# First tiles begun behind the first chunk's shift, the second chunk's maxima moved into them

## The chip, the cores and the metric

The kernel runs on one core of one Trainium2 chip. The metric is the device time of one execution in microseconds (us). Engines are named as in the profile: PE is TensorE, DVE VectorE, ACT ScalarE, POOL GpSimd, SP SyncE (which here only issues DMAs).

## The reference

A block of a transformer over T = 4096 rows of D = 256, with 16 heads of 16:

```
x = x + attn(layernorm(x));  x = x + ffn_fp8(layernorm(x))
attn:  q, k, v = split(x @ Wqkv + b)
       soft = softmax(q k^T * scale + causal mask) v                (per head, 4096 x 4096)
       state_t = retention * state_{t-1} + Gamma * (v_t k_t^T) * scale ;  stp_t = (W_static + state_t) q_t
       alpha = sigmoid(gelu(x @ w1 + b1) @ w2 + b2)
       y = alpha * soft + (1 - alpha) * stp ;  return y @ out_w + out_b
```

Softmax with its maxima and the recurrence over 4096 steps are what the change touches.

## The kernel before

The program has three blocks: a prologue (layernorm, projections, the first maxima), the attention block, and a last block (merge, output projection, FFN). The change is in the attention block.

**Groups, chunks, tiles.** The 16 heads are four groups of four. The 4096 queries are eight chunks of 512 (`CH`), taken in the order `ORDER = (3, 4, 5, 6, 7, 2, 1, 0)`; `s` is the place in that order. Chunk c attends to key tiles of 128 keys, 4(c + 1) of them, so a group has 144 tiles (`TILES`): 16 for chunk 3, 20 for chunk 4, and so on. A tile computes four heads' scores on PE (step `scores`, L1349), their exponentials on ACT (L1465, 128x512 each), and two tiles later the product with the values on PE (`values`, L1376), into one PSUM bank for the chunk.

**Maxima and the shift.** The softmax subtracts a maximum per query before the exponential. It is found ahead: step `max` has PE form scores the other way round (L1311), and DVE reduces two banks at a time (L1512). One such reduction is a *pair*: two `max` steps, one for each half of the partitions. Chunk c has 16(c + 1) `max` steps, so 32 pairs for chunk 3 and 40 for chunk 4. Four PSUM banks hold two pairs. When a chunk's last pair is in, DVE folds them (`fold`, L1517), PE turns the result (`shift_turn`, L1434), DVE splits it in two f16 rows (`shift_split`, L1524 and L1527), and SP copies these into `Q_st` with four DMAs of 2 KB, eight rows each (L1159). The first `scores` of the chunk wait for those DMAs (`shift_loaded`).

**The recurrence.** 64 units for a group, in 16 batches of four. SP loads each unit's value rows, broadcast to all partitions (`v_exp`, 256 KB, L1125); POOL multiplies by k (L1219); ACT scales (`scale`, L1474); POOL adds, DVE scans a batch (`scan`, L1547), POOL weighs with q, and every second batch PE has a `burst` of 40 matmuls into one bank. A `lag` (L1385, L1481, L1209) is a small product for every fourth batch.

**The order.** Every engine walks the same list of steps and does its own part of each. `first_steps()` makes the list of the entrance, `group_steps()` that of a group, tile by tile, from a string of letters: S a score, M a `max` step, v and w the halves of the values, V both, R the recurrence's steps, U small moves:

```python
PLAIN_TILE = "USSMMvSSMMw"
BURST_TILE = "USSMMRMMSSMMV"
SCAN_TILE = "USSRvSSMMw"
LAG_TILE = "USSMMVSSMMR"
```

`recurrence_steps()` says at which tile each scan, burst, scale and v load stands. The `max` steps run `AHEAD` = 144 steps (two chunks, 3 and 4) ahead of the tiles: a group's tiles reduce the chunks from the third on and then the next group's first two. Only for group 0 the entrance must do chunks 3 and 4. Chunk 3's maxima are formed in the prologue; chunk 4's 40 pairs are in `first_steps()`, before tile 0 of group 0. SP's part of the entrance is, in this order: the k, q and v rows of the first batch and eight `v_exp`, `V_first` (values of the first five chunks, 680 KB), the queries of chunks 5 and 6, `K_st` and `V_g` for the long chunks, the queries of chunk 7, and then the first chunk's shift rows. All of these go through one queue (`q1`).

Keys lie in `K_first` (first five chunks) and `K_st`, whose rows between the data must hold the constant `SHIFT_UNIT`: POOL fills all of `K_st` at the block's start (L1283) before its first product, and DVE clears the output bank (L1554).

Of the kernel before, what the change touches and what calls it, by code (L numbers as in the profile page):

```python
# [52 lines left out]
ORDER = (3, 4, 5, 6, 7, 2, 1, 0)  # L53
# [5 lines left out]
TILES = sum(KEY_TILES)  # L59
# [69 lines left out]
def transfers(name):  # L129
    return 1 if name[0] == "v" else STACK_LOADS  # L130
# [14 lines left out]

def recurrence_steps(last):

    period = LAST_PERIOD if last else PERIOD
    moves, slots = {}, {}

    def add(at, t, *step):
        at.setdefault(max(t, 0), []).append(step)

    for B in range(N_BATCHES):
        t = period * B + SLOT_AT
        if B % 2 == 1:
            add(slots, t, "burst", 0, B // 2)
        for k in range(BATCH):
            if not (last and B + 2 >= N_BATCHES):
                at, when = (slots, t) if B % 2 == 1 else (moves, t + 1 + k)  # L160
                add(at, when, "scale", 0, BATCH * (B + 2) + k)
            if not (last and B + 3 >= N_BATCHES):
                add(moves, t + V_AFTER + k, "v_load", 0, BATCH * (B + 3) + k)
        if not (last and B + 1 >= N_BATCHES):
            add(slots, t, "scan", 0, B + 1)
    for b in range(1, N_SWEEPS + (0 if last else 1)):
        add(moves, period * (SWEEP_BATCHES * b - 5) + SLOT_AT + KQ_AFTER, "kq_load", 0, b)
        add(slots, period * (SWEEP_BATCHES * b - 3) + SLOT_AT + LAG_AFTER, "lag", 0, b)
    return moves, slots


def first_steps():

    loads = [("load", 0, name, n) for name in EARLY for n in range(transfers(name))]

    steps = [("load_units", 0, 0)] + [x for x in loads if x[2] not in (f"q{ORDER[0]}", f"q{ORDER[1]}", "k_first")]
    release = None
    for s, n in ITEMS[:AHEAD]:
        if s > 0:
            steps.append(("max", 0, s, n))  # L180
        if release and n == 8:
            steps.append(release)
        if s > 0 and n == MAXES[s] // 4:
            steps += [("lag", 0, 0, 2), ("lag_evac", 0, 0, 2)]
        if n == MAXES[s] - 1:
            steps += [("fold", 0, s), ("shift_turn", 0, s, s)]
            release = ("shift_split", 0, s, s)
    if release not in steps:
        steps.append(release)
    steps += [("scale", 0, n) for n in range(BATCH)] + [("scan", 0, 0)]  # L190
    steps += [("scale", 0, BATCH + n) for n in range(BATCH)]
    steps += [("v_load", 0, 2 * BATCH + n) for n in range(BATCH)]
    return steps


def group_steps(last, pending, turns, used):

    steps = []
    todo = [(0,) + x for x in ITEMS[AHEAD:]] + ([] if last else [(1,) + x for x in ITEMS[:AHEAD]])
    rotation = list(range(S_BANKS))  # L200
    moves, slots = recurrence_steps(last)

# [49 lines left out]
    for s in range(NCH):  # L252
        for kt in range(KEY_TILES[s]):
# [87 lines left out]
def preln_attention_ffn_kernel(nc, x, wqkv, bqkv, out_w, out_b, w_static, lam, gamma, gate_w1,  # L341
                               gate_b1, gate_w2, gate_b2, ffn_wt, ffn_b, out):
    ctx = ExitStack()
    with ctx:
# [711 lines left out]
        with att:  # L1056
# [20 lines left out]
            with nc.Block() as block:  # L1077
# [115 lines left out]
                def _(pool):  # L1193
# [100 lines left out]
                def _(pe):  # L1294
# [160 lines left out]
                def _(act):  # L1455
# [44 lines left out]
                def _(dve):  # L1500
# [460 lines left out]
```

## Time and profile before

| | before |
|---|---|
| median of 3 runs | 1769.96 us (1768.66 to 1770.38) |
| the profiled execution | 1767.19 us |
| its span in the trace | 1765.5 us |
| attention block's first instructions | about 162.5 us |
| first exponential (tile 0 of group 0) | 211.44 us |
| busy in the span | PE 1625.4 (92%), DVE 1534.4 (87%), ACT 1394.8 (79%), POOL 1219.2 (69%) us |
| granted TensorE clock, mean | 0.955 |

The span is what the trace shows from the first to the last instruction; the execution's own time is 1.7 us longer. Busy shares are means over the program: the stretches below tell what holds the work in each. In a row of the timeline the number in brackets is the engine's idle time before it, and what ended it. A clock of 0.50 is 1.2 GHz, 1.00 is 2.4 GHz.

### The profile page before, as it was taken

How to read it: one execution, taken by the hardware profiler on the slowest of the kernel's cores; microseconds unless marked ns; L12 is line 12 of the kernel's file. 1: busy time of each engine (PE TensorE's matmuls, PEld its weight loads, DVE VectorE, ACT ScalarE, POOL GpSimd, SP SyncE). 2: the span in 40 equal slices, each digit the busy share in tenths (PEclk: the TensorE clock that was granted, in tenths of full speed). 3: DMA queues.
4: the chain of work that ended last, by engine and by line, in shares of the span. 5: the costliest groups of instructions: out<-in, count | busy, mean ns of one | idle time of the engine just before them, and what ended most of it. 6: DMA issues, size and time to landing. Idle time of an engine off the chain costs nothing. (4 is left out here: it accounts for less than half of the span.)

```text
span 1765.5 us, 44702 instructions
## 1 busy us (share of the span) xinstructions
PE 1625.4 (92%) x17582; PEld 583.6 (33%) x17582; DVE 1534.4 (87%) x1744; ACT 1394.8 (79%) x2839; POOL 1219.2 (69%) x1151
## 2 busy tenths in 40 slices
PE   5995699999999999999999999999999999999655
PEld 3541123233333332333333233233333332333532
DVE  6668989999899999998999999988999999940688
ACT  3651288998987899989888989998888889899234
POOL 3102497778777777787777777877778888880555
PEclk9995599999999999999999999999999999999886
DMA  5784343142212422232124222322242321200712
GB/s 162 252 254 144 77 108 87 58 99 75 74 60 82 112 70 76 73 81 77 63 79 111 65 84 70 98 60 71 85 115 64 97 73 60 69 16 11 244 48 95
DMA packets 115347, 163.22 MB, mean 92 GB/s; under 512 B 30081, under 2 KB 57793, under 8 KB 115137
## 3 DMA queue, kind: packets, MB, share of 16 engines
q1 hardware_dynamic: 112608, 158.74, 30.7%
q8 instruction: 137, 2.24, 0.6%
q10 hardware_dynamic: 2528, 1.64, 0.3%
q14 instruction: 74, 0.60, 0.1%
HBM read 121.87 MB, written 38.01 MB: 91 GB/s over the span
## 5 line engine op out<-in xcount | busy, mean ns | idle before, releaser
L1512 DVE TENSOR_REDUCE pmax<-PS 128x2 f32<-128x1024 f32 (+2 forms) x1120 | 1204.3, 1130 | 84.5 <-PE PS L1311 66.8
L1465 ACT ACTIVATE probs<-PS 128x512 f32<-128x512 f32 (+3 forms) x2304 | 1149.8, 575 | 155.5 <-PE PS L1349 76.5
L1376 PE MATMUL PS<-probs,V_g 128*17 128x256 f32 (+3 forms) x5064 | 395.8, 385 | 4.1 <-ACT o_t L1486 3.7
L1219 POOL TENSOR_TENSOR v_exp<-v_exp,k_rows 128x512 f32<-128x512 f32 x256 | 322.5, 1289 | 26.5 <-DMA v_exp<-qkv_t 26.2
L1349 PE MATMUL PS<-Q_st,K_st 50*128 50x512 f16 (+3 forms) x1408 | 288.8, 364 | 8.0 <-ACT probs L1465 6.6
L1261 POOL TENSOR_TENSOR state<-odd,q_rows 128x514 f32<-128x514 f32 x256 | 282.0, 1134 | 6.1
L1311 PE MATMUL PS<-K_st,Q_st 48*128 48x512 f16 (+3 forms) x1408 | 272.6, 357 | 0.3
L1376 PE MATMUL PS<-probs,V_first 128*17 128x256 f32 (+2 forms) x3296 | 264.9, 393 | 2.2 <-ACT o_t L1486 2.2
L1349 PE MATMUL PS<-Q_st,K_first 50*128 50x512 f16 (+3 forms) x896 | 194.1, 379 | 11.9 <-ACT probs L1465 6.0
L1311 PE MATMUL PS<-K_first,Q_st 48*128 48x512 f16 (+1 forms) x832 | 178.8, 391 | 19.6 <-DVE pmax L1512 19.4
L1250 POOL COPY carry<-odd 128x4 f32<-128x4 f32 x64 | 12.1, 188 | 252.7 <-DVE odd L1547 252.7
L1349 PEld LDWEIGHTS PS<-Q_st,K_st 50*128 50x128 f16 x1408 | 80.3, 93 | 295.4 <-ACT probs L1465 240.8
L1229 POOL TENSOR_TENSOR pairs<-pairs,v_exp 128x512 f32<-128x512 f32 x128 | 162.8, 1294 | 0.0
L1376 PEld LDWEIGHTS PS<-probs,V_g 128*17 128x17 f32 x5064 | 84.0, 95 | 185.6 <-issue 110.7
L1474 ACT ACTIVATE pairs<-v_exp,decay 128x256 f32<-128x256 f32 x256 | 128.6, 543 | 9.7 <-POOL v_exp L1219 9.7
L1349 PEld LDWEIGHTS PS<-Q_st,K_first 50*128 50x128 f16 x896 | 51.8, 93 | 208.9 <-ACT probs L1465 158.2
L1376 PEld LDWEIGHTS PS<-probs,V_first 128*17 128x17 f32 x3296 | 54.7, 95 | 144.2 <-issue 89.8
L1255 POOL TENSOR_TENSOR odd<-odd,pairs 128x512 f32<-128x512 f32 x64 | 96.7, 1510 | 5.0
L714 PE MATMUL PS<-xn_t,w_parts 128*128 128x512 f16 x336 | 84.0, 409 | 9.2 <-DVE xn_t L896 9.1
L1547 DVE TENSOR_TENSOR_SCAN odd<-decay_x,sums 128x516 f32<-128x516 f32 x64 | 82.2, 1285 | 10.9 <-POOL sums L1240 10.9
L1240 POOL TENSOR_TENSOR sums<-sums,pairs 128x512 f32<-128x512 f32 x64 | 82.9, 1296 | 5.0
L1409 PE MATMUL PS<-state,sum_e 128*32 128x256 f32 x1024 | 77.5, 394 | 0.0
(194 smaller groups left out, 1488.5 us busy)
## 6 DMA issues: line engine op xcount, KB each, us to landing
v_exp<-qkv_t SPq DMA_DIRECT2D x256, 256.0 KB
qkv_t<-proj SPq DMA_DIRECT2D x24, 512.0 KB, 4.7
qk_parts<-parts SPq DMA_DIRECT2D x16, 512.0 KB, 5.5
Q_st<-qk_parts SPq DMA_DIRECT2D x192, 32.0 KB, 3.7
v_rows<-vaug SPq DMA_DIRECT2D x8, 544.0 KB, 6.5
xin<-x SPq DMA_DIRECT2D x8, 512.0 KB, 6.4
k_rows<-qkv_t SPq DMA_DIRECT2D x16, 256.0 KB, 4.1
q_rows<-qkv_t SPq DMA_DIRECT2D x16, 256.0 KB, 6.5
```

Of the source, the lines that this page charges most:

```text
L714: mm = pe.matmul(PS[:, PROJ_BANK + u % 2, :], w, xn_t[:, par, x_part, c, :], start=(c == 0 and n == 0), stop=(c == HALF - 1 and n == len(S ...
L1219: pool.tensor_tensor(v_exp[:, n % RING], v_exp[:, n % RING], k_rows[:, b % 2], ALU.mult)\
L1229: pool.tensor_tensor(pairs[:, B % 2, k:k + 2], pairs[:, B % 2, k:k + 2], v_exp[:, slot:slot + 2, 1:CH:2], ALU.add).then_inc(pair_made, 1)
L1240: pool.tensor_tensor(own[:, :, 1:], own[:, :, 1:], pairs[:, B % 2, :, 1:PAIR:2], ALU.add)\
L1255: pool.tensor_tensor(middle, middle, pairs[:, B % 2, :, 0:PAIR:2], ALU.add).then_inc(middle_made, 1)
L1261: pool.tensor_tensor(state[:, B % STATES, k].rearrange("p (c e) -> p c e", e=PLACES), own[:, k, 0:PAIR + 1].unsqueeze(2).broadcast_to([P, ...
L1311: mm = pe.matmul(PS[:, bank, 0:width], Q_st[rows, c, pair, j * P:(j + 1) * P], keys[rows, pair, blk * CH:blk * CH + width], start=True, st ...
L1349: mm = pe.matmul(PS[:, bank, 0:CH - r * P], keys[rows, pair, kt * P:(kt + 1) * P], Q_st[rows, c, pair, r * P:CH], start=True, stop=(kt < T ...
L1376: mm = pe.matmul(PS[h * VW:h * VW + VN, out_bank(g, s), first:end], v[:, kt, h * VN:(h + 1) * VN], probs[:, tile % P_SLOTS, h, first - r * ...
L1465: act.activation(probs[:, tile % P_SLOTS, h, 0:CH - r * P], PS[:, step[5], 0:CH - r * P], ACT.Exp, scale=SCORE_SCALE).then_inc(exp_done, 1)
L1474: act.activation(pairs[:, B % 2, s % BATCH, :], v_exp[:, s % RING, 0:CH:2], ACT.Identity, scale=decay[:, 0, col:col + 1]).then_inc(u_scale ...
L1512: dve.tensor_reduce(pmax[:, s % 2, pair * TPC + j:GH * TPC:PAIRS * TPC, blk], PS[:, bank:bank + SIDES, 0:width], AX.X, ALU.max).then_inc(m ...
```

## The change

1. `first_steps()` does the fold and turn of chunk 3's maxima, then only the first 16 `max` steps (8 pairs) of chunk 4, eight of them on either side of the lag. The rest of chunk 4 (64 `max` steps, 32 pairs) goes to the tiles of group 0.
2. On SP, chunk 3's shift rows are copied right behind `V_first`, before the queries and long keys.
3. In group 0, 33 odd plain tiles have a third pair (`DENSE_TILE`), up to tile 77. By the end of tile 79 the maxima stand where they stood.
4. The first scan, the scales and v loads of the second and third batch go into tiles 1 to 6, and the first scans of group 0 stand 5, 3 and 1 tiles later; one lag 3 tiles later.
5. POOL no longer fills `K_st`, DVE no longer clears the bank: ACT does both at its start, with an Identity activation from a broadcast column.
6. Two waits of PE ahead of group 0 go, and the bank rotation starts at 2.

```diff
+TURN_COVER = 8
+AHEAD_FIRST = MAXES[0] + 2 * TURN_COVER
+FIRST_SCAN, LATE_BY, LATE_LAG = 2, 5, 3
 PLAIN_TILE = "USSMMvSSMMw"
+DENSE_TILE, MORE = "USSMMvMMSSMMw", 2
...
-def recurrence_steps(last):
+def recurrence_steps(last, first):
...
+    if first:
+        for k in range(BATCH):
+            add(moves, FIRST_SCAN + k, "v_load", 0, 2 * BATCH + k)
+            add(moves, FIRST_SCAN + 1 + k, "scale", 0, BATCH + k)
+        add(slots, FIRST_SCAN, "scan", 0, 0)
     for B in range(N_BATCHES):
-        t = period * B + SLOT_AT
+        t = period * B + SLOT_AT + (max(LATE_BY - 2 * B, 0) if first else 0)
...
 def first_steps():
-    steps = [("load_units", 0, 0)] + [x for x in loads if x[2] not in (f"q{ORDER[0]}", f"q{ORDER[1]}", "k_first")]
-    release = None
-    for s, n in ITEMS[:AHEAD]:
-        if s > 0:
-            steps.append(("max", 0, s, n))
-        if release and n == 8:
-            steps.append(release)
...
-        if n == MAXES[s] - 1:
-            steps += [("fold", 0, s), ("shift_turn", 0, s, s)]
-            release = ("shift_split", 0, s, s)
-    if release not in steps:
-        steps.append(release)
-    steps += [("scale", 0, n) for n in range(BATCH)] + [("scan", 0, 0)]
-    steps += [("scale", 0, BATCH + n) for n in range(BATCH)]
-    steps += [("v_load", 0, 2 * BATCH + n) for n in range(BATCH)]
+    maxima = [("max", 0, s, n) for s, n in ITEMS[MAXES[0]:AHEAD_FIRST]]
+    return ([("load_units", 0, 0)] + [x for x in loads if x[2] == "v_first"]
+            + [("fold", 0, 0), ("shift_turn", 0, 0, 0)] + maxima[:TURN_COVER] + [("shift_split", 0, 0, 0)]
+            + [x for x in loads if x[2] != "v_first"]
+            + [("lag", 0, 0, 1), ("lag_evac", 0, 0, 1)] + maxima[TURN_COVER:] + [("scale", 0, n) for n in range(BATCH)])
...
 def group_steps(last, pending, turns, used):
+    first = not pending
+    ahead = AHEAD_FIRST if first else AHEAD
+    behind = AHEAD - ahead + (MORE if first else 0)
+    todo = [(0,) + x for x in ITEMS[ahead:]] + ([] if last else [(1,) + x for x in ITEMS[:AHEAD]])
...
+            if order is PLAIN_TILE and t % 2 == 1 and behind:
+                order, behind = DENSE_TILE, behind - MORE
...
-                    pool.memset(K_st[:, :, :], SHIFT_UNIT).then_inc(ones_ready, 1)
...
-                    pe.wait_ge(turn_emptied, TURN_CREDIT + len(FIRST_TURNS))
-                    pe.wait_ge(lag_emptied, STEP_LAGS + FIRST_LAGS)
...
+                    act.activation(PS[:, O_BANK, :], neg_half[:, 0:1].broadcast_to([P, CH]), ACT.Identity, scale=0.0)\
+                        .then_inc(ones_ready, 1)
+                    act.activation(K_st[:, :, :].rearrange("p a t -> p (a t)"), neg_half[:, 0:1].broadcast_to([P, PAIRS * T]),
+                                   ACT.Identity, scale=-2 * SHIFT_UNIT).then_inc(ones_ready, 1)
...
-                    dve.memset(PS[:, O_BANK, :], 0.0).then_inc(ones_ready, 1)
```

The order that comes of it, at three places. SP at the block's start, before (`Q_st<-shift` are the shift rows, four transfers for a chunk, and `v_exp` behind them the third batch's values):

```order
L1125 DMA v_exp<-qkv_t 128x1x512 x8
L1097 DMA V_first<-v_rows 128x1360
L1106 DMA Q_st<-qk_parts 16x2x512 x12
L1106 DMA K_st<-qk_parts 16x2x1536 x6
L1097 DMA V_g<-v_rows 128x816
L1106 DMA Q_st<-qk_parts 16x2x512 x6
L1159 DMA Q_st<-shift 1x8x128 x8
L1125 DMA v_exp<-qkv_t 128x1x512 x4
```

and with the change:

```order
L1127 DMA v_exp<-qkv_t 128x1x512 x8
L1099 DMA V_first<-v_rows 128x1360
L1161 DMA Q_st<-shift 1x8x128 x4
L1108 DMA Q_st<-qk_parts 16x2x512 x12
L1108 DMA K_st<-qk_parts 16x2x1536 x6
L1099 DMA V_g<-v_rows 128x816
L1108 DMA Q_st<-qk_parts 16x2x512 x6
L1116 DMA k_rows<-qkv_t 128x512
```

The first chunk's four transfers moved from behind 25 loads to behind `V_first`; the second chunk's four come only with tile 14. DVE from its first fold on, before (`pmax` rows are pairs, x the number of pairs, and the scan is printed as SCALAR_TENSOR_TENSOR odd):

```order
L1517 TENSOR_REDUCE neg_max<-pmax 128x16
L1512 TENSOR_REDUCE pmax<-PS 128x2 x4
L1524 TENSOR_SCALAR shift<-PS 16x128
L1527 SCALAR_TENSOR_TENSOR shift<-PS,shift 16x128
L1512 TENSOR_REDUCE pmax<-PS 128x2 x36
L1517 TENSOR_REDUCE neg_max<-pmax 128x16
L1524 TENSOR_SCALAR shift<-PS 16x128
L1527 SCALAR_TENSOR_TENSOR shift<-PS,shift 16x128
L1547 SCALAR_TENSOR_TENSOR odd<-decay_x,sums 128x516
```

and with the change:

```order
L1520 TENSOR_REDUCE neg_max<-pmax 128x16
L1515 TENSOR_REDUCE pmax<-PS 128x2 x4
L1527 TENSOR_SCALAR shift<-PS 16x128
L1530 SCALAR_TENSOR_TENSOR shift<-PS,shift 16x128
L1515 TENSOR_REDUCE pmax<-PS 128x2 x9
L1550 SCALAR_TENSOR_TENSOR odd<-decay_x,sums 128x516
L1515 TENSOR_REDUCE pmax<-PS 128x2 x16
L1550 SCALAR_TENSOR_TENSOR odd<-decay_x,sums 128x516
L1515 TENSOR_REDUCE pmax<-PS 128x2 x11
L1520 TENSOR_REDUCE neg_max<-pmax 128x16
```

Of the 36 pairs behind the first split four still stand ahead of tile 0; the other 32 lie between the scores of tiles 0 to 13, and the fold comes behind them. PE there (L1312 is a `max` step, L1350 a score, L1377 values), from the last pairs of the entrance into tiles 0, 1 and 2:

```order
L1312 MATMUL PS<-K_first,Q_st 128x512 x6
L1350 MATMUL PS<-Q_st,K_first 128x512 x2
L1312 MATMUL PS<-K_first,Q_st 128x512 x2
L1350 MATMUL PS<-Q_st,K_first 128x512 x2
L1312 MATMUL PS<-K_first,Q_st 128x256
L1321 MATMUL PS<-mask_qk_sides,ident_sides 128x128 x2
L1312 MATMUL PS<-K_first,Q_st 128x256
L1321 MATMUL PS<-mask_qk_sides,ident_sides 128x128 x2
L1350 MATMUL PS<-Q_st,K_first 128x512 x2
L1312 MATMUL PS<-K_first,Q_st 128x512 x4
L1350 MATMUL PS<-Q_st,K_first 128x512 x2
```

Tile 0 is plain with two pairs; tile 1 has four `max` steps in a row between its scores, where a plain tile has two.

## Rows read from the trace of the kernel before

**Rows 1.** The page: busy time by engine, and its costliest group.

```profile
PE 1625.4 (92%) x17582; PEld 583.6 (33%) x17582; DVE 1534.4 (87%) x1744; ACT 1394.8 (79%) x2839; POOL 1219.2 (69%) x1151
L1512 DVE TENSOR_REDUCE pmax<-PS 128x2 f32<-128x1024 f32 (+2 forms) x1120 | 1204.3, 1130 | 84.5 <-PE PS L1311 66.8
```

**Rows 2.** Windows: stretch, its length, busy us by engine, clock, DMA share, GB/s.

```profile
162.50:174.10 11.60, 6.12 (x29) 1.39 (x29) 10.48 (x14) 0.00 (x0) 11.39 (x8) 0.50 0.73 205
174.10:209.40 35.30, 20.12 (x86) 4.74 (x86) 32.96 (x32) 5.41 (x10) 11.93 (x12) 0.50 0.38 80
209.40:211.44 2.04, 1.00 (x5) 0.49 (x6) 1.51 (x4) 0.00 (x0) 0.00 (x0) 0.50 0.00 0
211.44:413.30 201.86, 196.57 (x2174) 58.95 (x2171) 189.16 (x181) 179.82 (x365) 164.28 (x155) 0.97 0.35 93
413.30:574.46 161.16, 158.49 (x1965) 56.57 (x1959) 147.67 (x158) 138.70 (x295) 127.42 (x122) 1.00 0.22 67
```

**Rows 3.** Windows of three plain tiles and of one burst tile (columns as above).

```profile
237.72:244.47 6.75, 6.75 (x82) 1.78 (x80) 6.63 (x7) 6.51 (x12) 6.62 (x7) 1.00 0.16 60
246.97:252.17 5.20, 5.20 (x72) 2.41 (x70) 4.46 (x5) 3.81 (x9) 3.86 (x5) 1.00 0.02 5
```

**Rows 4.** Timeline of DVE at the entrance: start us, length us, instructions.

```profile
164.14 4.62 DVE L1512 TENSOR_REDUCE pmax<-PS 128x2 f32<-128x1024 f32 x4 [1.04 <-PE PS L1311]
168.98 0.28 DVE L1527 SCALAR_TENSOR_TENSOR shift<-PS,shift 16x128 f16<-16x128 f32 x1
169.19 5.53 DVE L1512 TENSOR_REDUCE pmax<-PS 128x2 f32<-128x256 f32 x6
176.50 15.99 DVE L1512 TENSOR_REDUCE pmax<-PS 128x2 f32<-128x1024 f32 x15 [1.79 <-PE PS L1311]
192.90 16.49 DVE L1512 TENSOR_REDUCE pmax<-PS 128x2 f32<-128x1024 f32 x15 [0.40 <-PE PS L1311]
209.42 0.24 DVE L1517 TENSOR_REDUCE neg_max<-pmax 128x16 f32<-128x80 f32 x1
210.65 1.21 DVE L1547 TENSOR_TENSOR_SCAN odd<-decay_x,sums 128x516 f32<-128x516 f32 x1
211.93 2.49 DVE L1512 TENSOR_REDUCE pmax<-PS 128x2 f32<-128x1024 f32 x2
```

**Rows 5.** Timeline of SP's queue at the entrance, issue times.

```profile
169.33 0.61 SPq L1097 DMA_DIRECT2D V_first<-v_rows  x1
183.10 2.75 SPq L1159 DMA_DIRECT2D Q_st<-shift  x4
```

**Rows 6.** Timeline of POOL at the entrance; ACT's group of 4096 columns.

```profile
162.81 6.92 POOL L1283 MEMSET K_st<- 128x8192 f16 x1
170.49 4.93 POOL L1219 TENSOR_TENSOR v_exp<-v_exp,k_rows 128x512 f32<-128x512 f32 x4
L849 ACT ACTIVATE decay_x<-decay 128x4096 f32<-128x4096 f32 x1 | 3.6, 3607 | 0.0
```

**Rows 7.** DMA: all Q_st loads, V_first, the issue at 172.32; busy tenths 186.0 to 189.9.

```profile
DMA to landing us min/median/max: 1.7/3.7/16.0
...
V_first<-v_rows SPq DMA_DIRECT2D x1, 680.0 KB, 17.2
...
DMA to landing us min/median/max: 16.0/16.0/16.0
...
DMA  5555657646386571591195514653645263645455
```

**Rows 8.** Windows: first eight tiles of groups 0 and 1, and a fall of the clock.

```profile
211.44:235.55 24.11, 21.46 (x172) 4.94 (x173) 18.75 (x17) 18.38 (x36) 23.08 (x22) 0.77 0.70 158
574.46:594.23 19.77, 18.42 (x193) 5.09 (x193) 18.88 (x24) 18.55 (x38) 13.43 (x13) 1.00 0.53 117
226.10:229.50 3.40, 1.89 (x23) 0.68 (x27) 3.40 (x4) 2.76 (x7) 3.40 (x3) 1.00 0.99 198
229.50:233.00 3.50, 3.50 (x26) 0.52 (x24) 2.53 (x3) 2.38 (x5) 3.42 (x4) 0.51 0.60 156
```

More of the change, by code:

```diff
@@ L167, in recurrence_steps @@
         add(moves, period * (SWEEP_BATCHES * b - 5) + SLOT_AT + KQ_AFTER, "kq_load", 0, b)
-        add(slots, period * (SWEEP_BATCHES * b - 3) + SLOT_AT + LAG_AFTER, "lag", 0, b)
+        late = LATE_LAG if first and b == 1 else 0
+        add(slots, period * (SWEEP_BATCHES * b - 3) + SLOT_AT + LAG_AFTER + late, "lag", 0, b)
     return moves, slots
 def first_steps():
-    loads = [("load", 0, name, n) for name in EARLY for n in range(transfers(name))]
-    steps = [("load_units", 0, 0)] + [x for x in loads if x[2] not in (f"q{ORDER[0]}", f"q{ORDER[1]}", "k_first")]
@@ L177, in first_steps @@
-    release = None
-    for s, n in ITEMS[:AHEAD]:
-        if s > 0:
-            steps.append(("max", 0, s, n))
-        if release and n == 8:
-            steps.append(release)
-        if s > 0 and n == MAXES[s] // 4:
-            steps += [("lag", 0, 0, 2), ("lag_evac", 0, 0, 2)]
-        if n == MAXES[s] - 1:
-            steps += [("fold", 0, s), ("shift_turn", 0, s, s)]
-            release = ("shift_split", 0, s, s)
-    if release not in steps:
-        steps.append(release)
-    steps += [("scale", 0, n) for n in range(BATCH)] + [("scan", 0, 0)]
@@ L191, in first_steps @@
-    steps += [("scale", 0, BATCH + n) for n in range(BATCH)]
-    steps += [("v_load", 0, 2 * BATCH + n) for n in range(BATCH)]
-    return steps
+    loads = [("load", 0, name, n) for name in EARLY for n in range(transfers(name))
+             if name not in (f"q{ORDER[0]}", f"q{ORDER[1]}", "k_first")]
+    maxima = [("max", 0, s, n) for s, n in ITEMS[MAXES[0]:AHEAD_FIRST]]
[3 more added lines that the diff above has]
+            + [("lag", 0, 0, 1), ("lag_evac", 0, 0, 1)] + maxima[TURN_COVER:] + [("scale", 0, n) for n in range(BATCH)])
@@ L196, in group_steps @@
 def group_steps(last, pending, turns, used):
     steps = []
-    todo = [(0,) + x for x in ITEMS[AHEAD:]] + ([] if last else [(1,) + x for x in ITEMS[:AHEAD]])
+    first = not pending
+    ahead = AHEAD_FIRST if first else AHEAD
+    behind = AHEAD - ahead + (MORE if first else 0)
+    todo = [(0,) + x for x in ITEMS[ahead:]] + ([] if last else [(1,) + x for x in ITEMS[:AHEAD]])
     rotation = list(range(S_BANKS))
-    moves, slots = recurrence_steps(last)
+    moves, slots = recurrence_steps(last, first)
@@ L279, in group_steps @@
             pending.append((0, s, kt))
-    assert not todo and max(slots) < TILES and max(moves) < TILES
+    assert not todo and not behind and max(slots) < TILES and max(moves) < TILES
     if last:
@@ L324 @@
 FIRST_STEPS = first_steps()
-STEPS, left = [], ([], [], 0)
+STEPS, left = [], ([], [], 2)
 for group in range(NG):
@@ L333 @@
 STEP_LAGS = N_SWEEPS
-FIRST_EMPTIED = emptied_before(FIRST_STEPS, {})[0]
-EMPTIED, tail = [], {}
+FIRST_EMPTIED, tail = emptied_before(FIRST_STEPS, {})
+EMPTIED = []
 for steps in STEPS:
```

## The prediction

> **What bounds the kernel now.** I read the page first: TensorE is busy 92% of the span, VectorE 87% (with 1204 us of maxima alone), ScalarE 79% [rows 1]. No engine is far behind, so the stretches decide. The windows show three of them around the change [rows 2]. From 162.5 to 209.4 only VectorE is full: 10.48 of 11.60 us and then 32.96 of 35.30, while ScalarE does 5.4 us in all and TensorE, at the 1.2 GHz level (granted clock 0.50), waits for banks. That is what the change attacks. From 211.44 on, tile follows tile. For the first 80 tiles (320 exponentials, 211.44 to 413.30) VectorE works 189.16 of 201.86 us, so it has only 12.7 us free; for the 64 tiles after them 147.67 of 161.16. Three plain tiles alone show how even the load is: 6.75 us, TensorE 6.75, VectorE 6.63, ScalarE 6.51 [rows 3]. A plain tile is held by all three at about 2.2 us. Last I read VectorE's and SyncE's timelines through the entrance [rows 4, 5].
>
> **What the change does not do.** It removes no reduction. The 32 pairs of the second chunk (chunk 4) that leave the entrance come back in the tiles: 33 odd plain tiles reduce three pairs where they reduced two. So the question is not how early the tiles start, but how much time VectorE is idle from 162.5 to the end of tile 79, where both orders have reduced the same 199 pairs (before 40 and 159, now 8 and 191). Before, that idle time is 11.60 - 10.48 + 35.30 - 32.96 + 2.04 - 1.51 + 12.70 = 16.7 us [rows 2]. That is the most that can be won. From tile 80 on nothing changes but bank numbers: taken at nothing.
>
> **Term 1, when tile 0 can start.** It needs the first chunk's shift rows in SBUF, four products and scalings of the recurrence, and ones_ready. VectorE's split is ready at 169.26 in both kernels, behind its first four pairs [rows 4]. SyncE then is just past V_first (issued 169.33, 0.61 us), so the four shift transfers go out at about 170.0 to 172.7 instead of 183.10 to 185.85 [rows 5]. The other conditions: four products end at 175.42, having begun behind GpSimd's fill of K_st (6.92 us) [rows 6], and four scalings follow, half a microsecond behind their product if ScalarE is free. Without the fill the products begin when the v rows land, so this chain ends by about 175.5. The fill on ScalarE, priced by its nearest row, 4096 columns in 3.61 us [rows 6], takes 7.2 us plus 0.6 for the PSUM bank, and ends near 171 on an engine that did nothing before 174.1 [rows 2]. Removing VectorE's memset saves 0.5 us, which four pairs behind the same start leave as nothing. All of this hides under the landing of the shift rows.
>
> That landing is the price the trace does not show directly, so I bound it. From below: the fastest transfer into Q_st lands 1.7 us after issue [rows 7], so 173.7, and the products would rule with 176. From above: eleven transfers of 256 KB and V_first with 680 KB are in the queue ahead. V_first takes 17.2 us from issue, to 186.5; the Q_st transfer issued at 172.32, the place in the queue that the last shift transfer will have, takes 16.0 us, to 188.3 [rows 7]. And from 186.0 to 189.9 the DMA engines are about half busy all along: about half of them still work off their queue while the others are done [rows 7]. I take the upper end, because the row nearest to the new transfers, in queue and in time, is that one; some of the congestion (Q_st and K_st loads) now comes behind, so 187.3 for the landing and 188.0 for the first exponential. Tile 0 starts 23.4 us earlier, not 35.
>
> The Trainium skill (DMA: Bandwidth & Descriptors, the cost components of one DMA) gives a transfer some 2.0 us of fixed cost and says the rest scales with size. By it alone 2 KB of shift rows would land near 174.7, and the products would start the tiles at 176: the sum below would then end 12 us lower. The 17.2 and 16.0 us of rows 7 speak against using it for a transfer behind a full queue.
>
> **Term 2, what VectorE must do from there to the end of tile 79.** Rows 4 give 38.25 us for the 36 pairs and the fold behind the first split (5.53 + 15.99 + 16.49 + 0.24). Four of those pairs stay ahead of the tiles (4/6 of 5.53, so 3.7 us): 34.5 us move in. With them come the second split (0.56) and the first scan (1.21): 36.3 us. Added to the 189.2 us of the tiles that is 225.5; recorded reductions overlap a little back to back (mean of one 1130 ns [rows 1], while 15 in a chain take 15.99 us), so I take 224.
>
> TensorE and ScalarE hide under this: an odd and an even tile have five pairs, 5.5 us at 1.1 each, where ScalarE needs 4.3 and TensorE 4.5 plus 0.4 for the extra pair.
>
> **Term 3, VectorE's idle time inside the tiles.** The first reduction starts 0.5 us after the first exponential [rows 4]. The first eight tiles of group 0 take 24.11 us with VectorE idle 5.4, against 19.77 and 0.9 in group 1 [rows 8]: TensorE starts at half clock and GpSimd is late. GpSimd's part goes, since the change puts the early scans later; I keep 2.5 us. The four tiles with a burst (TensorE 5.2 us without a pause) leave VectorE idle, 0.7 us in the one shown [rows 3]: 3 to 4 us for four, 3.5 taken. New: the shift of chunk 4 is turned behind tile 14 and needed at tile 16. The split waits for it behind tile 14's two pairs; from there four issues (the last starts 2.1 us after the first) and 1.7 us to land are 3.8 us, while VectorE has the three pairs of tile 15, 3.3 us, to do, and then TensorE must refill a bank: 1.3 us. Whatever is queued behind that wait on TensorE (tile 16 and its burst) moves with it. Another 1.2 us for output turns and uneven pairs. Together 9 us; bounds 4 and 18.
>
> **The sum.** 188.0 + 224 + 9 = 421 against 413.3: 8 us slower. In terms: the start gives 23.4, and 80 tiles take 233 instead of 201.9. The idle time that was to be won (16.7) comes back as a wait of some 14 us between the eighth pair (near 174) and tile 0, plus the 9. The profiled execution took 1767.19 us, span 1765.5; it becomes 1775. The median shown is 1769.96, 2.8 above it, so the forecast for the median is **1778**. A difference of 0.2%, 3.5 us, is about what a measurement of this kernel tells from none.
>
> **Rivals.**
> 1. *The shift rows land early* (faster). If the engines that carry eight-row transfers have drained, or small transfers slip past, the tiles start at 176 with the scalings and the sum is 176.5 + 224 + 9 = 409.5, that is 4 us faster: 1766. It decides if the landing is before some 176; at 180 there is no difference. For it: the first half of the engines is idle earlier [rows 7]. Against it: the v_exp loads that fill the queue also have eight source rows each. Chance 0.12. It is what the fixed cost in the Trainium skill (DMA: Bandwidth & Descriptors, the cost components of one DMA) alone would give.
> 2. *No difference.* The queue drains faster without Q_st and K_st loads beside it (landing at 184), and VectorE loses only 6 us in the tiles: 184.7 + 224 + 6 = 414.7, +1.4, so 1771. Chance 0.15.
> 3. *TensorE loses its clock in the dense tiles* (much slower). The clock fell to half from 229.5 to 233.0 after a stretch with TensorE 1.89 of 3.40 us busy [rows 8], and I price one such stretch at 1.3 us: the first eight tiles, at a mean clock of 0.77, spent 2 x 0.23 x 24.11 = 11 us at half clock and cost 24.11 - 19.77 = 4.3 us more than group 1's, of which 3.4/11 is 1.3. Held back by VectorE, TensorE is less busy than in any tile now. Eight such stretches, or a longer stall at tile 16, add 10 us: 1788. Against it: with 4.9 of 5.5 us of work it stays busier than in that stretch. Chance 0.13.
>
> **How the numbers follow.** My forecast has 0.60. Its own range, from 4 to 15 us with the bounds of landing and idle time, is 1774 to 1785. For 8 in 10 the range reaches over rival 2 and most of rivals 1 and 3: 1767 to 1788. Faster by over 0.2%: most of rival 1, 0.10. Within 0.2%: rival 2 with the edges of rival 1 and of the forecast, 0.18. Slower: 0.72.
>
> **What would show it.** In the profile after: no VectorE memset and a fill of about 7 us on ScalarE at 163; the shift transfers issued at 170; the first exponential at 188, after a wait that ends with a DMA (at 176: rival 1); VectorE over 95% busy over the first 80 tiles, which take about 233 us; odd tiles near 3.3 us; a wait of TensorE of 1 to 2 us at the first scores of tile 16; granted clock 1.00 through the dense tiles (below it: rival 3); tiles 80 to 143 in 161 us and groups 1 and 2 in 359 us as before. I am wrong if tile 0 starts before 180, or if the 80 tiles take under 225 us: then the dense tiles cost less than their VectorE work, and the reading of rows 2 fails.

## The result, and the profile after

The changed kernel takes **1784.7 us** (median of 8 runs, 1776.0 to 1786.8), the kernel before 1770.2 (median of 8 beside them, 1768.7 to 1774.1). The ratio is 1.0072 with an interval of 1.0056 to 1.0087, about 12.7 us slower (the two medians stand 14.5 apart). Forecast were 1778, 8 us slower, with a range of 1767 to 1788: the direction was right, and the loss came out about one and a half times the forecast.

The profiled execution took 1784.49 us, with a span of 1782.7 (before 1767.19 and 1765.5). The page shows the engines' work unchanged, and more waiting in the maxima than the 84.5 us of [rows 1]:

```profile
PE 1626.1 (91%) x17590; PEld 587.5 (33%) x17590; DVE 1534.6 (86%) x1743; ACT 1404.2 (79%) x2841; POOL 1209.0 (68%) x1150
L1515 DVE TENSOR_REDUCE pmax<-PS 128x2 f32<-128x1024 f32 (+2 forms) x1120 | 1203.7, 1130 | 104.6 <-PE PS L1312 83.4
```

The windows, with the columns of [rows 2]: the entrance, tiles 0 to 79, tiles 80 to 143, group 1, and then two stretches at half clock.

```profile
164.70:190.12 25.42, 6.49 (x27) 1.80 (x28) 9.12 (x11) 11.06 (x9) 16.55 (x18) 0.50 0.79 187
190.12:427.62 237.50, 214.47 (x2275) 65.95 (x2272) 221.75 (x216) 183.14 (x370) 163.88 (x156) 0.94 0.31 81
427.62:588.78 161.16, 158.51 (x1963) 56.45 (x1959) 147.68 (x158) 138.70 (x296) 126.00 (x121) 1.00 0.22 67
588.78:947.60 358.82, 352.06 (x4154) 115.60 (x4152) 336.69 (x345) 318.76 (x661) 278.86 (x265) 1.00 0.29 80
234.30:241.10 6.80, 4.97 (x52) 2.33 (x50) 2.91 (x4) 2.77 (x6) 3.71 (x5) 0.53 0.01 2
299.30:309.50 10.20, 8.43 (x52) 1.99 (x54) 6.91 (x7) 5.83 (x11) 3.19 (x3) 0.51 0.13 39
```

Against [rows 2] the time went as follows. The block starts 2.2 us later (164.7 for 162.5), lost in the prologue, which the change doesn't touch: 1.7 us of it stand ahead of the first fall of the clock (at 38.4 before, at 40.1 now, with 94 matmuls done in both), and the falls behind it, up to 140 us, add up to the same 13.6 us in both. From the block's start to the first exponential it takes 25.4 us, before 48.9: 23.5 us won. The 80 tiles take 237.5 us, before 201.9: 35.6 lost. Tiles 80 to 143 take what they took (161.16), and so do groups 1 and 2, 358.8 us each for 359.0 and 358.9. From group 3 on 3.2 us are lost, 2.4 of them early in that group behind one more stretch at half clock (1309.7 to 1316.5), which runs 1 and 5 below show too and the others don't. From block start to the end of tile 79, where the change acts, it is 262.9 us instead of 250.8: **12.1 us lost**, as large as the measured difference.

SyncE's queue and ScalarE at the entrance, to compare with [rows 5] and [rows 6]:

```profile
166.52 6.33 SPq L1127 DMA_DIRECT2D v_exp<-qkv_t  x8
172.90 0.46 SPq L1099 DMA_DIRECT2D V_first<-v_rows  x1
173.40 2.74 SPq L1161 DMA_DIRECT2D Q_st<-shift  x4
```

```profile
164.56 0.60 ACT L1494 ACTIVATE PS<-neg_half 128x512 f32<-128x512 f32 x1 [20.83 <-PEq L510]
165.10 7.01 ACT L1496 ACTIVATE K_st<-neg_half 128x8192 f16<-128x8192 f32 x1
...
178.17 0.53 ACT L1473 ACTIVATE pairs<-v_exp,decay 128x256 f32<-128x256 f32 x1 [1.26 <-POOL v_exp L1221]
178.72 1.28 ACT L1464 ACT_TABLE_LOAD   x1
190.12 2.07 ACT L1464 ACTIVATE probs<-PS 128x512 f32<-128x512 f32 x4 [10.12 <-PE PS L1350]
```

The shift rows are issued 8.7 us after the block's start (173.40). ScalarE is ready at 180.0, after its last scaling and a load of its table (`ACT_TABLE_LOAD`, 1.28 us); then it waits 10.1 us. The waits of the 80 tiles tell who for (engine and line, awaited; total us, times, longest):

```profile
PEld PS L1312 <- DVE pmax L1515: 47.7, 100, 1.3
ACT probs L1464 <- PE PS L1350: 44.2, 56, 10.1
DVE pmax L1515 <- PE PS L1312: 26.6, 20, 15.7
PE PS L1350 <- DMA Q_st<-shift: 19.9, 3, 16.2
```

TensorE waits three times for shift rows: 16.2 us at tile 0 and 1.8 each at tiles 16 and 36. The first scores at 189.50 come 13.3 us after the last shift transfer went out (its issue began at 175.5 and took 0.65). Here is tile 15 into 16, the timeline of all engines with the rows between left out:

```profile
229.25 0.23 DVE L1520 TENSOR_REDUCE neg_max<-pmax 128x16 f32<-128x80 f32 x1
229.41 2.35 DVE L1515 TENSOR_REDUCE pmax<-PS 128x2 f32<-128x1024 f32 x2
231.67 0.27 DVE L1527 TENSOR_SCALAR shift<-PS 16x128 f16<-16x128 f32 x1
232.28 2.73 SPq L1161 DMA_DIRECT2D Q_st<-shift  x4
232.69 0.45 ACT L1464 ACTIVATE probs<-PS 128x128 f32<-128x128 f32 x2 [1.43 <-PE PS L1321]
236.22 0.61 PE L1350 MATMUL PS<-Q_st,K_first 50*128 50x512 f16 x2 [1.83 <-DMA Q_st<-shift]
236.84 1.09 ACT L1464 ACTIVATE probs<-PS 128x512 f32<-128x512 f32 x2 [3.71 <-PE PS L1350]
237.24 0.43 DVE L1515 TENSOR_REDUCE pmax<-PS 128x2 f32<-128x256 f32 x1 [1.59 <-PE PS L1321]
```

The fold comes at 229.25, the split behind two pairs at 231.67, the four issues take 2.7 us, and the scores that need them run at 236.22. At about 234.7, three tenths of a microsecond into TensorE's wait for these rows (234.39 to 236.22), the granted clock falls to half and stays there for 6.8 us, which hold tile 16 and its burst. So the fall doesn't come of that wait alone: tile 15 had already made TensorE wait 0.40 and 0.78 us for VectorE, and in the stretch just ahead of the fall it was busy 1.80 of 3.40 us. The same is seen ahead of the fall in tile 35:

```profile
231.30:234.70 3.40, 1.80 (x23) 0.50 (x18) 3.37 (x6) 0.45 (x2) 3.40 (x4) 1.00 0.01 1
296.20:299.60 3.40, 1.60 (x18) 0.42 (x18) 3.37 (x5) 0.45 (x2) 3.32 (x3) 0.99 0.28 96
```

Tiles 15 and 16 took 6.0 and 6.9 us, where the tiles of the kernel before took 2.4 and 2.2, and one with a burst 5.2 [rows 3].

**The account of VectorE's idle time.** Before, 16.7 us from block start to the end of tile 79. After: 25.42 - 9.12 = 16.3 in the entrance and 237.50 - 221.75 = 15.75 in the tiles, 32.1 us, 15.4 more. Its recorded work in the same stretch falls by 3.2 us (234.1 to 230.9; why the same 199 pairs are recorded shorter, I did not follow), and 15.4 - 3.2 = 12.2 is the loss.

### The profile page after: what moved, and what is told of

Its sections match the earlier page's. It is cut to its first block and busy times, and to the rows that moved or that the text cites. A ratio compares the mean times of both kernels' runs of the same rounds, so it can differ in the third digit from the quotient of the medians.

```text
span 1782.7 us, 44718 instructions
## 1 busy us (share of the span) xinstructions
PE 1626.1 (91%) x17590; PEld 587.5 (33%) x17590; DVE 1534.6 (86%) x1743; ACT 1404.2 (79%) x2841; POOL 1209.0 (68%) x1150
## 5 line engine op out<-in xcount | busy, mean ns | idle before, releaser
L1377 PE MATMUL PS<-probs,V_g 128*17 128x256 f32 (+3 forms) x5064 | 396.0, 385 | 3.7 <-ACT o_t L1485 3.3
L1350 PE MATMUL PS<-Q_st,K_st 50*128 50x512 f16 (+3 forms) x1408 | 287.9, 364 | 8.4 <-ACT probs L1464 6.1
L1312 PE MATMUL PS<-K_st,Q_st 48*128 48x512 f16 (+3 forms) x1408 | 272.9, 359 | 11.1 <-DVE pmax L1515 10.5
L1377 PE MATMUL PS<-probs,V_first 128*17 128x256 f32 (+2 forms) x3304 | 266.7, 395 | 1.6 <-ACT o_t L1485 1.6
L1350 PE MATMUL PS<-Q_st,K_first 50*128 50x512 f16 (+3 forms) x896 | 192.6, 383 | 29.1 <-DMA Q_st<-shift 19.9
L1312 PE MATMUL PS<-K_first,Q_st 48*128 48x512 f16 (+1 forms) x832 | 172.5, 378 | 8.7 <-DVE pmax L1515 7.4
L1350 PEld LDWEIGHTS PS<-Q_st,K_st 50*128 50x128 f16 x1408 | 80.1, 93 | 291.4 <-ACT probs L1464 235.3
L1377 PEld LDWEIGHTS PS<-probs,V_g 128*17 128x17 f32 x5064 | 84.0, 95 | 182.5 <-issue 110.9
L1350 PEld LDWEIGHTS PS<-Q_st,K_first 50*128 50x128 f16 x896 | 51.5, 93 | 216.6 <-ACT probs L1464 147.6
L1377 PEld LDWEIGHTS PS<-probs,V_first 128*17 128x17 f32 x3304 | 54.9, 95 | 138.1 <-issue 88.6
L1312 PEld LDWEIGHTS PS<-K_st,Q_st 48*128 48x128 f16 x1408 | 70.4, 94 | 47.3 <-DVE pmax L1515 33.4
```

The costliest lines, as they stand in the source:

```text
L1312: mm = pe.matmul(PS[:, bank, 0:width], Q_st[rows, c, pair, j * P:(j + 1) * P], keys[rows, pair, blk * CH:blk * CH + width], start=True, st ...
L1350: mm = pe.matmul(PS[:, bank, 0:CH - r * P], keys[rows, pair, kt * P:(kt + 1) * P], Q_st[rows, c, pair, r * P:CH], start=True, stop=(kt < T ...
L1377: mm = pe.matmul(PS[h * VW:h * VW + VN, out_bank(g, s), first:end], v[:, kt, h * VN:(h + 1) * VN], probs[:, tile % P_SLOTS, h, first - r * ...
```

## The experiments

**What has to be told apart.** Theory: the loss has two causes. (A) The shift rows of the first chunk lie in the queue behind 3.4 MB (eleven transfers of 256 KB, V_first), so VectorE runs out of its eight pairs and waits. (B) The second chunk's turn, now behind tile 14, comes too late for tile 16, and the third chunk's, behind 34, too late for 36; TensorE waits and works at half clock around it. Rivals: the dense tiles are slow by themselves (TensorE held back, not VectorE full), or the fills on ScalarE cost something. In every profile I read two numbers: block start to first exponential, and the length of tiles 0 to 79. That cuts off the prologue and the tail, which differ by a stretch or two at half clock from run to run.

**1. The shift rows ahead of V_first and of four v_exp.** The whole change otherwise.

```diff
-                                for n in range(RING):
+                                for n in range(BATCH):
                                     load_v_exp(g, n)
...
-    return ([("load_units", 0, 0)] + [x for x in loads if x[2] == "v_first"]
-            + [("fold", 0, 0), ("shift_turn", 0, 0, 0)] + maxima[:TURN_COVER] + [("shift_split", 0, 0, 0)]
+    return ([("load_units", 0, 0)]
+            + [("fold", 0, 0), ("shift_turn", 0, 0, 0)] + maxima[:TURN_COVER] + [("shift_split", 0, 0, 0)]
+            + [x for x in loads if x[2] == "v_first"] + [("load_more", 0, 0)]
```

> The changed kernel, with only four v_exp loads (not eight) ahead of the first chunk's shift rows, and V_first and the other four behind them. Theory (the shift rows wait in the queue behind 3.4 MB): they land by about 179, tile 0's first exponential moves from 190.1 to about 178 to 180, and the whole is 10 to 12 us faster than the changed kernel (median near 1774). The waits at tiles 16 and 36 stay. Rival (something else holds tile 0 back, the recurrence's products or the fill on ScalarE): tile 0 stays near 188 to 190 and the time within 2 us of the changed kernel's 1784.7.

Measured: 1773.4 us against 1770.4, ratio 1.002 (1.001 to 1.003), so 11.3 us under the changed kernel. TensorE's wait for the rows at tile 0, in the waits of 160 to 185, and the two windows (entrance, tiles 0 to 79):

```profile
PE PS L1354 <- DMA Q_st<-shift: 3.4, 1, 3.4
```

```profile
164.20:178.80 14.60, 7.31 (x28) 1.80 (x28) 10.27 (x12) 11.00 (x8) 7.85 (x10) 0.50 0.63 200
178.80:416.30 237.50, 213.63 (x2271) 66.10 (x2272) 221.13 (x216) 183.17 (x370) 174.22 (x165) 0.94 0.33 88
```

The wait shrinks from 16.2 to 3.4 us, the entrance from 25.4 to 14.6, and the tiles don't change at all (237.5). (A), the place in the queue, is shown, at 10.8 us. The same four transfers of 2 KB, with seven of 256 KB ahead of them (1.8 MB) and not 3.4 MB, are used 3.3 us after the last issue instead of 13.3 (scores at 176.57, issues 170.56 to 173.31). ScalarE then sets the first exponential, as rival 1 had it: the last scaling ends at 177.57, the table load takes 1.28 us, and the exponential follows at 178.88. That is 14.7 us after the block's start, where rival 1 had 13.5: it had no table load.

**2. Twenty pairs in the entrance.** The wait stays, but VectorE works through it; 21 dense tiles are left, and the turns move to tiles 9 and 29.

```diff
-AHEAD_FIRST = MAXES[0] + 2 * TURN_COVER
+AHEAD_FIRST = MAXES[0] + 40
```

> The changed kernel with 20 pairs of the second chunk in the entrance instead of 8 (21 dense tiles instead of 33); order of DMAs unchanged. Theory (time follows VectorE's idle time, and the wait for the shift rows is idle time that pairs can fill): tile 0 stays at 189 to 191, VectorE's 12 pairs fill 13 us of the wait, the second chunk's shift is turned at tile 9 and the third's at 29, so the waits at tiles 16 and 36 go too (6 us): 1764 to 1768, 2 to 6 us faster than the kernel before. Rival (dense tiles cost by TensorE or ScalarE, not by VectorE's work): 12 dense tiles fewer give back about 12 x 0.4 = 5 us only, so about 1780.

Measured: **1761.15 us**, ratio 0.995 (0.9931 to 0.997): faster than both kernels, and 3 us under the 1764 to 1768 that were expected.

```profile
164.00:187.60 23.60, 14.13 (x63) 3.62 (x64) 21.92 (x23) 11.21 (x9) 16.41 (x19) 0.50 0.77 198
187.60:404.30 216.70, 203.35 (x2239) 62.08 (x2236) 209.82 (x205) 182.29 (x370) 163.69 (x156) 0.98 0.35 89
```

VectorE idles 1.7 us in the entrance and 6.9 in the tiles, 8.6 in all against 16.7 before: 8.1 us less, and 9.2 were measured. There is no stall at tiles 16 or 36, since the twelve pairs more in the entrance also bring the turns five tiles forward. So this run alone doesn't part (A) from (B); runs 1 and 4 do. The shift rows came a little earlier too: the first scores stand 23.0 us after the block's start, in the changed kernel 24.8, with the same order of transfers.

**3. Dense tiles without their third reduction's work.** Of the third pair only one column is reduced. The kernel leaves out the maxima of 33 pairs, so that its time is that of less VectorE work with the same instructions.

```diff
-DENSE_TILE, MORE = "USSMMvMMSSMMw", 2
+DENSE_TILE, MORE = "USSMMvNNSSMMw", 2
...
+                                if len(step) > 4:
+                                    width = 1
```

> The changed kernel with the third pair of each dense tile reduced over its first column only: the reduction of 33 pairs is left out, TensorE's work and the order are whole. Theory (VectorE bounds the dense tiles): an odd tile falls from some 2.9 to 3.3 us to 2.3 to 2.5, the first 80 tiles from 237 to about 208, the whole to about 1755. Rival (TensorE's extra matmuls, or the clock it loses, bound them): the 80 tiles stay above 225 us and the whole above 1772.

Measured: 1774.5 us, ratio 1.0024 (1.0013 to 1.0035). The theory missed and the rival came true: the tiles took 229.3 us, not 208, and both of its numbers (over 225 and over 1772) hold.

```profile
190.90:420.20 229.30, 211.49 (x2275) 62.92 (x2272) 192.22 (x216) 182.73 (x370) 165.15 (x156) 0.94 0.32 83
```

VectorE works 29.5 us less and the tiles are only 8.2 us shorter. So VectorE's work is not all that sets a dense tile. The stalls of (B) are still there (tiles 15, 16 and 35 took 5.6, 7.1 and 5.6 us), and tile 45 shows the other thing. Here is that tile in the changed kernel, then in this run, with the plain tile behind it:

```profile
327.52:330.91 3.39, 2.80 (x32) 0.77 (x28) 3.39 (x4) 2.17 (x4) 3.31 (x4) 1.00 0.02 5
324.01:326.98 2.97, 2.69 (x32) 0.69 (x28) 2.52 (x4) 2.17 (x5) 2.89 (x4) 1.00 0.02 6
326.99:329.18 2.19, 2.19 (x26) 0.50 (x24) 2.19 (x3) 2.17 (x4) 2.19 (x3) 1.00 0.00 0
```

In the changed kernel VectorE is busy all through the tile, 3.39 of 3.39 us. With the third reduction thinned it has time left, yet the tile is only 0.4 us shorter: TensorE now works 2.69 us, 0.5 more than in the plain tile, and still waits 0.3. The wait is in the timeline of tile 53:

```profile
347.55 0.39 PE L1314 MATMUL PS<-K_st,Q_st 48*128 48x512 f16 x2
348.49 0.34 PE L1314 MATMUL PS<-K_st,Q_st 48*128 48x384 f16 x2 [0.33 <-DVE pmax L1519]
349.02 4.58 DVE L1519 TENSOR_REDUCE pmax<-PS 128x2 f32<-128x768 f32 x4 [0.53 <-PE PS L1323]
349.86 2.79 ACT L1466 ACTIVATE probs<-PS 128x512 f32<-128x512 f32 x5 [0.58 <-PE PS L1352]
```

Four banks hold two pairs. Two pairs in a row on TensorE mean that the second waits for banks that VectorE is still reading, and the scores behind them come late, so ScalarE idles too. With the third reduction as good as free, tiles 45 and 47 still took 3.0 and 2.9 us between plain ones of 2.2; with the whole reduction they take 3.4. So a dense tile costs about 0.7 us more than a plain one even if VectorE has time: 0.3 to 0.5 us are TensorE's own work for the extra pair, since a plain tile leaves it no pause, and 0.3 to 0.4 its waits for banks. No run varied the number of banks, so that part rests on the timeline.

**4. The turns two tiles earlier.** Even plain tiles below 12 are dense as well, so the second chunk's turn comes behind tile 12 and the third's behind 32, and as many fewer tiles are dense later.

```diff
-            if order is PLAIN_TILE and t % 2 == 1 and behind:
+            if order is PLAIN_TILE and (t % 2 == 1 or t < 12) and behind:
```

> The changed kernel with the same 33 dense tiles, but the even plain tiles 0, 4, 6, 8 and 10 among them, so that the second and third chunk's shifts are turned at tiles 12 and 32 instead of 14 and 34. VectorE's work up to tile 80 is the same. Theory (two waits for shift rows, each with a fall of TensorE's clock behind it, are what my forecast missed): no wait for a DMA at tiles 16 and 36, the clock stays at 1.00 there, 4 to 8 us faster than the changed kernel (1777 to 1781). Rival (VectorE is the bound and works through those waits): the idle time only moves, within 2 us of 1784.7.

Measured: 1773.88 us, ratio 1.0022 (1.0013 to 1.0032), 10.8 us under the changed kernel. TensorE's waits of 190 to 420 and the window of the tiles:

```profile
PE PS L1350 <- DMA Q_st<-shift: 15.9, 1, 15.9
```

```profile
191.30:419.90 228.60, 209.54 (x2275) 64.50 (x2271) 221.70 (x216) 183.17 (x370) 163.02 (x154) 0.97 0.33 83
```

One wait is left of three; tiles 15 and 16 take 2.9 and 4.7 us, tile 35 2.9; the clock doesn't fall there. VectorE's work is the same to 0.05 us, and the tiles are 8.9 us shorter. (B) is shown, as one thing: the late turns, with the waits and the falls that came with them. It gave more than the 4 to 8 us expected: two waits of 1.8 us go with a loss two and a half times as long.

**5. The fills alone.** The kernel before, with only the fills of `K_st` and of the bank moved to ScalarE (the change's two activations in, the memsets of POOL and DVE out).

> The kernel before with one part of the change alone: K_st and the output bank are filled by ScalarE instead of GpSimd and VectorE. My costing (hidden in both kernels): ScalarE does a fill of about 7 us from 163 on, the products start some 2.5 us earlier, and the time is that of the kernel before within 0.1%. Rival (the fill delays something on ScalarE or slows an engine beside it): 1 to 3 us slower.

Measured: 1770.9 us, ratio 0.9996 (0.9986 to 1.0006); entrance 48.5 us, tiles 201.1, as before (48.9, 201.9). The fills cost nothing and bring nothing where the entrance is long. This profile has the fall of the clock early in group 3 (1297.8 to 1304.6) without the rest of the change, so that fall is not the change's. The later scans (part 4 of the change) and the two waits of TensorE (part 6) were not run alone.

**6. Both causes taken away** (the edits of 1 and 4).

> The changed kernel with both repairs: the shift rows behind four v_exp loads, and the dense tiles in front. If the wait at the entrance and the waits at tiles 16 and 36 are separate causes, they add: 11.3 and 10.8 us, so 1762 to 1764. If VectorE's total work limits what both can give, less: 1766 to 1769.

Measured: 1764.38 us, ratio 0.9962 (0.9945 to 0.998).

```profile
164.40:178.30 13.90, 7.73 (x34) 2.23 (x34) 10.32 (x13) 11.04 (x9) 7.96 (x11) 0.50 0.64 204
178.30:408.10 229.80, 209.26 (x2266) 63.94 (x2266) 222.59 (x215) 183.12 (x369) 173.02 (x164) 0.97 0.35 92
```

The two gains add: 10.8 + 8.9 = 19.7 in the profiles alone, and here 262.9 - 243.7 = 19.2. The median stands 0.4 us above the 1762 to 1764 that were expected of causes that add. With both gone, the idea of the change is worth 6 us.

**7. The order of 1, and twelve pairs in the entrance** (`MAXES[0] + 24`), so that VectorE is full up to the rows' landing; 29 dense tiles, turns at 13 and 32.

> The changed kernel with the shift rows behind four v_exp loads, 12 pairs in the entrance instead of 8 and 29 dense tiles (the second and third chunk's shifts turned at tiles 13 and 32). Theory (time follows VectorE's idle time only, wherever the pairs stand): the same as the kernel with 20 pairs within 3 us, 1760 to 1764. Rival (a dense tile costs more than its VectorE work, as the thinned kernel suggests): eight dense tiles more than the kernel with 20 pairs, at 0.55 us each, 4 to 5 us slower than it, 1765 to 1767.

Measured: 1765.32 us, ratio 0.9976 (0.9964 to 0.9988).

```profile
164.90:179.30 14.40, 9.46 (x40) 2.34 (x40) 12.86 (x15) 11.05 (x9) 7.95 (x11) 0.50 0.62 201
179.30:409.70 230.40, 211.58 (x2261) 64.22 (x2260) 219.41 (x213) 182.66 (x370) 174.74 (x164) 0.95 0.35 91
228.00:231.40 3.40, 0.60 (x9) 0.09 (x1) 1.65 (x2) 1.68 (x4) 3.35 (x4) 1.00 0.00 0
231.60:238.40 6.80, 6.30 (x33) 1.16 (x33) 4.71 (x4) 4.07 (x8) 6.72 (x6) 0.51 0.39 121
```

The entrance is closed (1.5 us idle), but tile 16, with its burst, took 8.0 us. It isn't a wait for shift rows: these were issued at 219.57 to 222.3 and TensorE doesn't wait for them in any tile. Its one long wait, and the longest of ScalarE's that led to it, are

```profile
231.10 1.09 PE L1354 MATMUL PS<-Q_st,K_first 50*128 50x512 f16 x2 [2.80 <-ACT stp_sb L1494]
229.03 0.53 ACT L1477 ACTIVATE pairs<-v_exp,decay 128x256 f32<-128x256 f32 x1 [1.62 <-POOL v_exp L1225]
```

TensorE waits until ScalarE has emptied the burst's bank (`stp_sb`). ScalarE does that behind four scalings, and each of these waits for GpSimd's product. GpSimd had waited 3.8 us for `v_exp` loads up to there; in the changed kernel it waits for none in those tiles. Run 1's order sends four of these loads later, which may be the reason, but run 6 has the same order and no such stall, and nothing varied it alone. The clock falls at 231.4, behind the wait. VectorE idles 3.05 us up to 232.70. The median lies 1.3 us above what the theory gave and inside the 1765 to 1767 of the rival, but this stall stands in the way of reading it for either.

**8. The twenty pairs of 2, with the third pair at another place in the tile** (`"USSMMvSSMMMMw"`).

> The kernel with 20 pairs in the entrance, the third pair of a dense tile formed behind the second pair of scores and its pair of maxima instead of ahead of them, so that the first chunk of exponentials is fed earlier. Theory (VectorE's 5 pairs in two tiles bound them, 5.5 to 5.7 us, wherever the third stands): within 1.5 us of 1761. Rival (TensorE's order starves ScalarE, which the thinned kernel's 2.8 us tiles point to): 21 tiles gain 0.3 us each, 1754 to 1756.

Measured: 1763.49 us, ratio 0.9956 (0.9942 to 0.997); entrance 23.8, tiles 216.7, the same as in 2. The median is 2.3 us above run 2's, outside the 1.5 us expected but within the spread of the two (1758.98 to 1764.91 here, 1754.33 to 1767.30 there), and over 7 us from the rival's. Where the third pair stands makes no difference in the stretch: four `max` steps stand in a row either way, and the banks are two pairs deep.

The times from block start to the end of tile 79 beside the medians: kernel before 250.8 and 1770; change 262.9 and 1785; runs 1 to 4 252.2, 240.3, 254.5, 253.8 and 1773, 1761, 1775, 1774; runs 5 to 8 249.6, 243.7, 244.8, 240.5 and 1771, 1764, 1765, 1763. Against the kernel before, the medians follow this stretch to within 4 us.

## Why the prediction was right in direction and short in size

*What the change does not do* held: what counts is VectorE's idle time from the block's start to tile 79, and runs 2 and 6 gained by filling it (idle 8.6 and 10.8 us for 16.7). The rest of the kernel kept its 161.16 and 359 us.

*Term 1, when tile 0 can start* was right in its mechanism, and its number is partly luck. Forecast 23.4 us earlier, measured 23.5 from the block's start. But the shift rows were issued 8.7 us after the block's start and not 7.5 (the eight `v_exp` issues took 6.33 us for 5.22), and were used 13.3 us after the last issue, where the term had 14.6 to the landing: two errors of 1.2 us that cancel. Over the five profiles with this order of transfers (the change, runs 2, 3, 4 and 8) the first exponential stands 23.6 to 25.4 us after the block's start. The shift rows behind the queue came within a microsecond of the Q_st transfer at that place (used at 24.8 us after the block's start, landed at 25.8 [rows 7]), and the fill of 7.2 us on ScalarE (measured 7.01) lay hidden. Run 1 shows that it is the queue. The half-busy DMA engines of [rows 7] carry less than the prediction took from them: the share is a mean of 16 engines and doesn't tell that half of them were done. Rival 1 fell. The Trainium skill (DMA: Bandwidth & Descriptors, Anatomy of one DMA — SWDGE (gpsimd) path) gives its fixed 2.0 us for one transfer issued by GpSimd and says nothing of a queue. SyncE's 2 KB behind a full queue needed over 13 us here.

*Term 2, VectorE's work* was 221.75 us for 224, right. Its second sentence, that TensorE and ScalarE hide under it, held in the changed kernel where nothing stalls: tile 45 had VectorE busy all of its 3.39 us. It hides less than it seems to, though: by run 3 TensorE's work and its waits for banks hold a dense tile at 0.7 us over a plain one even with VectorE's third reduction gone. The sums of busy time for two tiles (5.5, 4.9 and 4.3 us) leave out these waits.

*Term 3, VectorE's idle time inside the tiles* is **the step that failed in size**: 15.75 us for 9. Over the tiles 15 and 16 (230.81 to 243.73) and 35 and 36 (295.32 to 304.43) VectorE idled 5.3 and 2.9 us:

```profile
230.81:243.73 12.92, 9.77 (x96) 3.58 (x94) 7.64 (x10) 5.13 (x13) 9.75 (x10) 0.74 0.01 3
295.32:304.43 9.11, 6.08 (x52) 1.69 (x52) 6.25 (x8) 2.96 (x8) 5.83 (x5) 0.73 0.30 98
```

That is 8.2 us, for which the term had 1.3 for the wait at tile 16 and about 0.9 for its burst; the other tiles idled 7.6, for some 6.8 in the term. The wait at tile 16 was priced well (1.8 us of TensorE, 1.6 of VectorE, for 1.3), but two things were not in the term: the third chunk's turn moves from 25 to 34 and makes the same wait at tile 36, and the clock falls around both, for 6.8 and 10.2 us. Run 4 puts the whole at 8.9 us of tile time, and without it VectorE idles 6.9 us in the tiles: the rest of the term was too large by some 1 us (7.7 us without the 1.3 for tile 16).

The sum: start as forecast, VectorE's work 2.2 under, its idle time 6.8 over, so 237.5 for 233, and with the start 35.6 - 23.5 = 12.1 us lost, where the prediction had 31.1 - 23.4 = 7.7. Of the 14.5 us between the medians the rest is the prologue and the tail, which differ from run to run.

*Rival 2* (no difference) fell with both of its conditions. *Rival 3* came in part: its "longer stall at tile 16" is what came, while the dense tiles of this trace, once TensorE has left half clock at 200.6, keep theirs outside the two falls. By its price, 1.3 us for 3.4, the 17 us of the two falls would be 6.5 us; with the two waits, 3.7, that makes an estimate of 10.2 for the 8.9 that run 4 measured, so the price is near but not shown. Its mechanism, TensorE less busy because VectorE holds it back, is seen once each in runs 4, 6 and 7, in tile 61 (rows in the last section).

Of the signs that the prediction named, TensorE's wait at tile 16 (1.83 us) and the 161 and 359 us of the rest came as written. VectorE was busy 93% of the first 80 tiles and not over 95%, and the dense tiles took 2.7 to 3.8 us around the 3.3, but for 15 and 35 with 6.0 and 5.9.

What stays open: how much of the 8.9 us of (B) is the waits themselves and how much the clock. Both vanish together in run 4. And why run 2 stands 3 us below run 6 in time: it has 12 dense tiles fewer, and no fall of the clock in its tiles where run 6 has one of 6.8 us in tiles 61 to 63; no run varied only that.

## What to carry to other kernels

When work moves from an idle stretch into full tiles, count the bounding engine's idle time in both orders: starting earlier gains nothing unless work fills the wait that remains (twenty pairs under the landing, which also brought the turns forward, won 9 us where eight lost 13). Look for every point whose lead over its consumer shrinks, not only the first: here the second chunk's turn went from the entrance to 2 tiles ahead of its use, and the third's from 11 tiles to 2, which was overlooked. And order a shared queue by who waits: four transfers of 2 KB behind 3.4 MB cost 11 us.

## What was not expected of the hardware

- A 2 KB transfer is served with the queue it stands in. With 3.4 MB ahead it was used 13.3 us after the last issue; with 1.8 MB ahead, 3.3 us (run 1). The Trainium skill (DMA: Bandwidth & Descriptors, Queues, rings and completion order) says that each engine takes its descriptors in ring order; these runs agree, as far as the time to use tells: no view here shows the order within an engine.
- TensorE fell from 2.4 to 1.2 GHz after stretches without a long wait. Ahead of the falls at 234.7 and 299.6 it was busy 1.80 and 1.60 of 3.40 us, with waits of up to 0.8 us and the first part of one of 1.8. In run 7 a wait of 2.80 us stood ahead of the fall at 231.4. Runs 4, 6 and 7 show one more fall each, of 3.4 to 6.8 us, in tile 61, where every wait is under a microsecond; ahead of it TensorE was busy 2.15, 2.15 and 2.14 of 3.40 us with VectorE busy all the time:

```profile
369.20:372.60 3.40, 2.15 (x28) 0.84 (x26) 3.40 (x5) 2.81 (x6) 3.16 (x3) 1.00 0.01 2
356.90:360.30 3.40, 2.15 (x26) 0.76 (x24) 3.40 (x4) 2.78 (x6) 2.81 (x3) 1.00 0.01 2
357.70:361.10 3.40, 2.14 (x30) 0.69 (x22) 3.40 (x4) 2.88 (x7) 3.40 (x4) 1.00 0.20 73
```

- ScalarE filled 8192 columns of f16 in 7.01 us, POOL 6.92 [rows 6]: for this fill the two are nearly equal, and ScalarE had nothing else to do.
